# Another order of the work from the last pair's transposes to the first expert slot, and the ranks in two fp32r passes

## The reference, cut to what matters

```
x = x + xattn(layernorm(x), ctx, ctx)        # softmax over 1601 context rows
x = x + attn(layernorm(x))                   # causal, 64 rows of a batch
x = layernorm(x)  -> ffn, added to x:
    top2 of sigmoid(x @ centroids.T + bias) over 8 experts, softmax of the two scores
    shared: 2 experts, gelu(x @ Wfc.T) @ Wproj.T
    routed: 8 experts, the same, weighted by the gates
```

## Time and profile before

| | |
|---|---|
| median of 3 executions | 253.61 us (253.21 to 254.71) |
| the profiled execution | 252.07 us |
| its span, first to last instruction | 250.3 us |
| outside the span | 1.8 us |
| TensorE busy | 242.9 us, 97% |
| VectorE, ScalarE, GpSimd busy | 61%, 55%, 20% |

### The profile page before, as it was taken

One profiled execution on the slowest core, in us unless ns is written; L12 is line 12 of the kernel. 1 busy time (PEld: TensorE's weight loads), 2 busy tenths in 40 slices (PEclk: granted clock), 3 DMA queues, 4 the chain that ended last, 5 costly groups with the idle time before them and its releaser, 6 DMA issues.

```text
span 250.3 us, 5122 instructions
## 1 busy us (share of the span) xinstructions
PE 242.9 (97%) x1908; PEld 209.6 (84%) x1908; DVE 152.4 (61%) x365; ACT 137.2 (55%) x271; POOL 50.6 (20%) x81
## 2 busy tenths in 40 slices
PE   7999999999999999999998999999999999999994
PEld 6857646366467599999998899999999999999994
DVE  1722246545635788788759147666766766667683
ACT  0725206052152688796776166666666666666641
POOL 5100000000100010420686002102122222226700
PEclk9999999999999999999999999999999999999999
DMA  7999999999999999930166358999989999920132
GB/s 249 425 432 402 417 415 427 384 405 429 351 376 385 352 347 429 427 143 0 67 187 261 101 152 283 373 356 369 370 346 358 363 360 364 335 107 21 56 135 84
DMA packets 13870, 74.12 MB, mean 296 GB/s; under 512 B 1524, under 2 KB 8444, under 8 KB 9500
## 3 DMA queue, kind: packets, MB, share of 16 engines
q1 hardware_dynamic: 12700, 70.59, 74.4%
q0 software_dynamic: 1008, 2.76, 2.9%
q10 hardware_dynamic: 144, 0.53, 0.6%
HBM read 67.56 MB, written 6.32 MB: 295 GB/s over the span
## 4 chain that ended last, share of the span: by engine, by line
PE 72%; DMA 15%; POOL 3%; DVE 3%; ACT 3%; issue 2%; SPq 1%; POOLq 0%; DVEq 0%; ACTq 0%
PE psum L512 64%; DMA raw<-experts_dram 9%; PE psum L760 4%; POOL slot_x_dram L479 3%; DMA slot_x_dram<-second,rows_of 3%; DMA squares<-squares_dram 2%; PE psum L601 1%; PE psum L778 1%; DMA xrow<-slot_x_dram 1%; ACT prob L885 1%; PE psum L821 1%; DVE xn L1046 1%; PE psum L552 0%; PE psum L650 0%; PE psum L692 0%
## 5 line engine op out<-in xcount | busy, mean ns | idle before, releaser
L512 PE MATMUL psum<-xrowT,ring 128*128 128x128 f32 x480 | 58.3, 275 | 0.0
L512 PEld LDWEIGHTS psum<-xrowT,ring 128*128 128x128 f32 x480 | 56.2, 192 | 0.0
L1301 DVE TENSOR_TENSOR dlo<-ring,dhi 128x1024 fp32r<-128x1024 f32 x30 | 38.4, 1281 | 3.7 <-ACT dhi L968 3.7
L1320 DVE TENSOR_TENSOR slot_hlo<-slot_h,slot_hhi 128x512 fp32r<-128x512 f32 x30 | 20.8, 692 | 30.0 <-ACT slot_hhi L996 30.0
L994 ACT ACTIVATE slot_h<-psum 128x512 f32<-128x512 f32 x30 | 18.0, 600 | 35.7 <-PE psum L512 35.7
L512 PE MATMUL psum<-dhi,slot_hhi 128*128 128x256 f32 x120 | 36.3, 302 | 0.1
L512 PE MATMUL psum<-dhi,slot_hlo 128*128 128x256 f32 x120 | 33.8, 282 | 0.0
L512 PE MATMUL psum<-dlo,slot_hhi 128*128 128x256 f32 x120 | 33.8, 282 | 0.0
L968 ACT ACTIVATE dhi<-ring 128x1024 fp32r<-128x1024 f32 x30 | 31.1, 1040 | 0.0
L504 POOL DMA_INDIRECT results_dram<-y_rows,result_row x13 | 15.6, 1199 | 71.8 <-DMA results_dram<-y_rows,result_row 55.3
L512 PE MATMUL psum<-xh,parted 128*128 128x256 f32 x128 | 26.8, 286 | 0.1
(11 more groups left out here) (195 smaller groups left out, 408.2 us busy)
## 6 DMA issues: line engine op xcount, KB each, us to landing
ring<-experts_dram SPq DMA_DIRECT2D x15, 2048.0 KB, 8.2
ctx<-ctx_dram SPq DMA_DIRECT2D x4, 3072.0 KB, 24.5
ctxT_start<-ctxT_start_dram SPq DMA_DIRECT2D x4, 2048.0 KB, 19.0
ctxT_rest<-ctxT_rest_dram SPq DMA_DIRECT2D x4, 1154.0 KB, 21.8
raw<-experts_dram SPq DMA_DIRECT2D x2, 2048.0 KB, 16.4
slot_x_dram<-empty_row SPq DMA_DIRECT2D x1, 1935.0 KB, 16.9
xrow<-slot_x_dram SPq DMA_DIRECT2D x15, 129.0 KB, 7.1
squares<-squares_dram SPq DMA_DIRECT2D x1, 1285.0 KB, 14.2
```

What stands on the lines that cost most here:

```text
L512: return pe.matmul(out, lhsT, rhs, start=first, stop=last)
L1301: dve.tensor_tensor(dlo[b % 2][:, steps, :], ring[b][:, steps, C * P:STEP_W], dhi[b % 2][:, steps, :].bitcast(F32), ALU.subtract).then_inc ...
L1320: dve.tensor_tensor(slot_hlo[:, half, :], slot_h[:, half, :], slot_hhi[:, half, :].bitcast(F32), ALU.subtract).then_inc(slot_hlo_ready, 1)
```

## The change

The removed part of the list stands in plan() above and is left out of the diff. The second half of the list, from pair 3's transposes to the first slot, is written in another order. "split" 0 stands ahead of pair 3's transposes, where it stood behind pair 2's projection; the value products W of pair 3 are cut at other places and end later in the list. Units, norms and routing entries change places by a few positions. SyncE's and GpSimd's programs keep their order, apart from three constants on GpSimd. The ranks are computed in two fp32r matmuls, the first over the running sums (with the total as a fifth block of 8 columns), the second over the choices; before, they were three fp32 matmuls.

```
--- before.py
+++ after.py
@@ -79,30 +79,30 @@
                   ("exp", t + 1, 2), ("exp", t + 1, 3), *([] if t else [("x_bias", )]), ("W", t, 3 if t else 4, KT)]
 
     t, c, late = T - 1, T - 2, T - 3
...
+    order += [("split", 0), ("T", t, 0), ("T", t, 1), ("mixT", c), ("probT", late), ("T", t, 2), ("z", late),
+              ("T", t, 3), ("proj", c), ("split", 1), ("W", t, 0, 1), ("norm2", c), ("norm3", late), ("W", t, 1, 4),
+              ("split", 2), ("W", t, 4, 6), ("split", 3), ("W", t, 6, 7), ("split", 4), ("xn2T", c), ("W", t, 7, 9),
+              ("split", 5), ("xn3T", late), ("tq", c), ("W", t, 9, 10), ("xl", late), ("W", t, 10, 11), ("sc", c),
+              ("W", t, 11, KT), ("split", 6), ("v", c), ("hid", 0), ("mixT", t), ("hid", 1), ("split", 7),
+              ("exp2", c), ("feat", 0), ("proj", t), ("hid", 2), ("hid", 3), ("feat", 1), ("feat", 2), ("probT", c),
+              ("norm2", t), ("down", 0), ("z", c), ("feat", 3), ("xn2T", t), ("split", 8), ("split", 9), ("hid", 4),
+              ("tq", t), ("down", 1), ("hid", 5), ("sc", t), ("norm3", c), ("feat", 4), ("down", 2), ("v", t),
+              ("split", 10), ("exp2", t), ("xn3T", c), ("hid", 6), ("probT", t), ("xl", c), ("route", 0), ("z", t),
+              ("route", 1), ("feat", 5), ("hid", 7), ("down", 3), ("norm3", t), ("split", 11), ("feat", 6),
+              ("down", 4), ("xn3T", t), ("xl", t), ("route", 2), ("down", 5), ("route", 3), ("feat", 7), ("hid", 8),
+              ("rz", ), ("down", 6), ("sigmoid", ), ("top2", ), ("indices", ), ("hid", 9), ("feat", 8), ("hot", ),
+              ("choices", ), ("feat", 9), ("down", 7), ("hid", 10), ("hid", 11), ("feat", 10), ("gap", ), ("down", 8),
+              ("hid", 12), ("feat", 11), ("hid", 13), ("rank", ), ("place", ), ("place_experts", ), ("down", 9),
+              ("place_rows", ), ("hid", 14), ("feat", 12), ("hid", 15), ("down", 10), ("down", 11),
+              ("place_tokens", ), ("gates", ), ("feat", 13), ("feat", 14), ("hid", 16), ("down", 12), ("hid", 17),
+              ("down", 13), ("down", 14), ("split", 12), ("feat", 15), ("feat", 16), ("feat", 17), ("hid", 18),
+              ("down", 15), ("hid", 19), ("down", 16), ("down", 17), ("feat", 18), ("split", 13), ("feat", 19),
+              ("split", 14), ("hid", 20), ("down", 18), ("split", 15), ("feat", 20), ("down", 19), ("hid", 21),
+              ("hid", 22), ("feat", 21), ("hid", 23), ("down", 20), ("slot_down", 0), ("hid", 24), ("feat", 22),
+              ("down", 21), ("down", 22), ("feat", 23), ("hid", 25), ("feat", 24), ("hid", 26), ("down", 23),
+              ("hid", 27), ("slot_down", 1), ("feat", 25), ("down", 24), ("down", 25), ("hid", 28), ("feat", 26),
+              ("feat", 27), ("down", 26), ("slot_rows", ), ("feat", 28), ("hid", 29), ("down", 27), ("down", 28),
+              ("tables", ), ("feat", 29), ("down", 29)]
     return order
 
 
@@ -118,7 +118,8 @@
         ident = sb("ident", [P, P])
         mask = sb("mask", [P, P])
         neghalf = sb("neghalf", [P, T])
-        tri = sb("tri", [P, P])
+        tri = sb("tri", [P, P], F32R)
+        ones_r = sb("ones_r", [P, P], F32R)
         ones = sb("ones", [P, P])
         iota8 = sb("iota8", [P, T, ROUTED])
         iota128 = sb("iota128", [P, ROUTED])
@@ -155,9 +156,8 @@
         idxf = sb("idxf", [P, T, TOP])
         hot = sb("hot", [P, TOP, T, ROUTED])
         gat = sb("gat", [P, TOP, T, ROUTED])
-        chosen = sb("chosen", [P, T, ROUTED])
-        before = sb("before", [P, T, ROUTED])
-        total = sb("total", [P, ROUTED])
+        chosen = sb("chosen", [P, T, ROUTED], F32R)
+        before = sb("before", [P, T + 1, ROUTED], F32R)
         rank = sb("rank", [P, T, ROUTED])
         count = sb("count", [P, ROUTED])
         over = sb("over", [P, 3, ROUTED])
@@ -430,8 +430,8 @@
                                     pattern=[[-1, P]], channel_multiplier=1))
             pool.memset(mask[SQ:P, 0:SQ], MASKED).then_inc(consts, 1)
             pool.wait_ge(consts, 4)
-            link(pool.memset(tri[:, :], 1.0))
-            pool.affine_select(out=tri[:, :], in_=tri[:, :], compare_op=ALU.is_ge, fill=0.0, base=-1,
+            pool.tensor_copy(ones_r[:, :], ones[:, :])
+            pool.affine_select(out=tri[:, :], in_=ones[:, :], compare_op=ALU.is_ge, fill=0.0, base=-1,
                                pattern=[[1, P]], channel_multiplier=-1).then_inc(consts, 1)
             link(pool.memset(empty_row[:, :], 0.0))
             pool.iota(empty_row[:, D:D + 1], pattern=[[0, 1]], base=TOP * N, channel_multiplier=1,
@@ -446,7 +446,7 @@
 
             link(pool.iota(xn[:, :, D], pattern=[[P, T]], base=0, channel_multiplier=1,
                            allow_small_or_imprecise_dtypes=True))
-            link(pool.memset(before[:, 0, :], 0.0))
+            link(pool.tensor_copy(before[:, 0, :], empty_row[:, 0:ROUTED]))
             link(pool.memset(ones8[:, :], 1.0))
             pool.iota(iota8[:, :, :], pattern=[[0, T], [1, ROUTED]], base=0, channel_multiplier=0,
                       allow_small_or_imprecise_dtypes=True).then_inc(consts, 1)
@@ -729,11 +729,10 @@
             def ranks():
 
                 pe.wait_ge(chosen_ready, 1)
+                mm(bank(RANK_BANK, 0, (T + 1) * ROUTED), ones_r[:, :], before[:, :, :].rearrange("p t e -> p (t e)"),
+                   True, False)
                 mm(bank(RANK_BANK, 0, T * ROUTED), tri[:, :], chosen[:, :, :].rearrange("p t e -> p (t e)"),
-                   True, False)
-                mm(bank(RANK_BANK, 0, T * ROUTED), ones[:, :], before[:, :, :].rearrange("p t e -> p (t e)"),
-                   False, True)
-                mm(bank(RANK_BANK, T * ROUTED, ROUTED), ones[:, :], total[:, :], True, True).then_inc(rank_ps, 1)
+                   False, True).then_inc(rank_ps, 1)
 
             def hidden(n, tok):
 
@@ -1222,10 +1221,12 @@
             def choices():
 
                 link(dve.tensor_tensor(chosen[:, :, :], hot[:, 0, :, :], hot[:, 1, :, :], ALU.add))
-                for t in range(1, T):
-                    link(dve.tensor_tensor(before[:, t, :], before[:, t - 1, :], chosen[:, t - 1, :], ALU.add))
-                dve.tensor_tensor(total[:, :], before[:, T - 1, :], chosen[:, T - 1, :], ALU.add
-                                  ).then_inc(chosen_ready, 1)
+                for t in range(1, T + 1):
+                    ins = dve.tensor_tensor(before[:, t, :], before[:, t - 1, :].bitcast(F32),
+                                            chosen[:, t - 1, :].bitcast(F32), ALU.add)
+                    if t < T:
+                        link(ins)
+                ins.then_inc(chosen_ready, 1)
 
             def place():
```

More of the change, by code:

```diff
@@ L81, in plan @@
     t, c, late = T - 1, T - 2, T - 3
[L82 to L105, removed]
```

## The result

The changed kernel takes **260.71 us** (median of 6 runs, 260.34 to 262.22). The kernel before took 253.94 (6 runs, 253.21 to 254.71) on the same chip. The ratio is 1.0279, with a 95% interval of 1.0249 to 1.0308: 6.8 us slower in the medians, 7.1 by the ratio. The forecast was 258.5, its range 255.6 to 260.4. So the direction and the main mechanism (the stall) were right, and the total was too small by 2.2 us, just outside the range.

The account below looks back on a forecast made before the run. TensorE, busy 242.9 of 250.3 us, was taken as the bound. To the median of 253.6 us came +4.1 from the order and ranks and +0.8 for the clock, +4.9 in all: 258.5 us, range 255.6 to 260.4.

Parts of the forecast that it names:

- the stall: Pair 3's transpose group 2 on TensorE waits for ScalarE's copy, held behind split 0 until raw[0] lands: +5.1 us.
- the small waits: TensorE's waits at pair 2's xn2T (-0.3), pair 3's xn3T (+0.3) and before the slots (-0.3, -0.3).
- the ranks: Two small fp32r instructions replace six rank instructions on TensorE: -0.4 us (-0.35 to -0.6).
- the clock: TensorE's clock may fall to half in the idle time ahead of group 2: +0.8 us, bounds 0 and 2.0.
- partial: Rival: raw[0] lands 1 to 3 us earlier, TensorE waits 2 to 4, clock holds; 254.7 to 256.6 us; chance 0.07.
- xn3T of pair 3: TensorE waits for pair 3's last norm, with too few units to fill the time: +0.3 us (0 to 0.6).
- xn2T: TensorE's 0.28 us wait ahead of pair 2's xn2T goes, both norms being done by then: -0.3 us.
- Before the slots: Waits at a down unit (0.65) and slot_rows (0.42) shrink: -0.3 (0 to -0.65) and -0.3 (-0.4 to +0.8) us.
- in time: Rival: raw[0] lands by about 77.3, so split 0 hardly delays group 2; -0.5 to -1.5, 252.5 us; chance 0.07.
- The routing chain becomes the bound: Rival: token rows come later, slot_rows waits 1 to 2 us on top; 260.5 to 261.5 us; chance 0.06.
- the ranks do not get cheaper: Rival: small fp32r rank instructions cost as much as the fp32 ones, +0.4 us on any case; no chance given.

Follow-up runs that it names:

- split 0 taken back: Changed kernel with split 0's list entry moved behind pair 2's proj, no longer ahead of pair 3's transposes; 254.67 us, ratio 1.0069.
- raw[0] first: Changed kernel with the load of raw[0] issued ahead of the last ctx block instead of behind it; 254.92 us, ratio 1.0052.
- the filler: Changed kernel with 17 unused fp32 identity matmuls on TensorE ahead of pair 3's transpose group 2; 259.08 us, ratio 1.0233.
- new head: Kernel before with the new order up to the rank, split 0 behind proj, and fp32r ranks; old order behind the rank; 255.04 us, ratio 1.0028.
- ranks alone: Kernel before in its old order, with only the ranks changed to two fp32r matmuls; 253.46 us, ratio 1.0025.
- new tail: Kernel before with the new order only behind the rank, splits 10 and 11 behind gates, and fp32r ranks; 253.17 us, ratio 0.9966.

## Why the forecast was right in kind and too small

The step that failed is the account of the order outside the stall. The forecast put the small waits and the ranks at -0.3 - 0.4 + 0.3 - 0.3 - 0.3 = -1.0 us; the changed kernel with split 0 taken back, which has all of them, is 1.7 us above the kernel before. That is 2.7 us off. The stall was 1.0 smaller than forecast (4.1 timed against 5.1), the clock 0.2 larger in the medians (about 1 against 0.8), and the kernel before took 0.3 us more in its six runs than the 253.6 that I started from: 2.7 - 1.0 + 0.2 + 0.3 = 2.2, the whole miss. In the profiled execution the clock was mis-sized as well, 2.7 us against 0.8.

The second profile of the kernel before is the better yardstick for the sum, as it has the late waits that 12 of the 13 profiles with all scatters have. Start times of TensorE in it and in three others, and the differences that follow:

| | W of pair 3 | to the rank | rank to slot_rows | slot_rows to last matmul | last matmul |
|---|---|---|---|---|---|
| before, second profile | 80.08 | 33.16 | 27.39 | 106.80 | 247.43 |
| after | 86.22 | 35.02 | 26.91 | 107.51 | 255.66 |
| split 0 taken back | 80.17 | 34.62 | 26.79 | 107.49 | 249.07 |
| raw[0] first | 80.98 | 34.33 | 26.84 | 107.50 | 249.65 |

After against before is +8.23 = 6.14 + 1.86 - 0.48 + 0.71. The 0.71 is no loss: one unit of 0.71 us moved behind slot_rows. The two profiled executions lie 8.24 us apart in time (261.08 and 252.84), the medians 6.8.

- **Split 0 ahead of the transposes, forecast +5.1: 4.4 in the trace, 4.1 timed.** Every step of it happened, and the size was 0.7 to 1.0 too large: the landing (81.22 against 81.86), the split, the copy behind it, group 2 behind that. The transfer was 0.9 us shorter than in the earlier trace rows, with a start 0.2 later. That it could not vanish, and that it would not be partial, held in both profiles of the changed kernel.
- **The clock, forecast +0.8 between 0 and 2.0: 2.7 us in the profiled execution** (1.7 in the second one, about 1 in the medians against the filler, 1.7 against the two executions without a fall). Two errors. I took the price of a fall as four microseconds of work; it was 5.4. And I halved it because one case of a fall proves little; the mean clock was 0.978 to 0.993 in all twelve executions of the changed kernel, and not one kept it whole (a late fall, seen in other kernels, may be all of it in some).
- **xn3T of pair 3, forecast +0.3 (0 to 0.6): 0.70 or 0.71**, in all seven profiles with the new head. From W to the rank the new head costs 34.62 - 33.16 = 1.46 us: this wait, 0.30 ahead of xn2T, and some 0.5 in smaller gaps and spacings that I did not foresee.
- **xn2T, forecast -0.3: this step failed too.** The second profile of the kernel before does not have this wait, so there was nothing to win, and without the stall the new head has it: 0.30 us with split 0 taken back, 0.59 with the new head alone.
- **The ranks, forecast -0.4: 0.45 in the trace, nothing to be seen in the time** (ratio 1.0025 alone). The late wait did not take it up in the trace: it was 2.16 us there and 2.19 in the second profile of the kernel before, and from W to the last matmul the ranks alone need 166.86 us against 167.35. That the timed runs don't show these 0.5 us may come from their more frequent falls of the clock; it is not shown.
- **Before the slots, forecast -0.6 in two terms: this step failed.** I read the 0.65 and the 0.42 as waits that a list could move. Both do disappear, and others take their place. Rank to slot_rows falls by 0.48, where one unit less (0.71) and the ranks (0.45) alone make 1.16: the new order loses 0.7 there. In this stretch the late release of TensorE's results during the scatters makes the waits, and I had not seen it because I had one profile of the kernel before, with none of it.

Against the second profile of before, then: 4.3 for the stall (82.41 against 78.09), 2.6 for the clock (1.8 ahead of W, 0.8 in it), 1.1 for the head (what is left of 1.86), -0.45 for the ranks and +0.7 for the tail, 8.25 in all. In the timed medians: stall 4.1, clock about 1, the rest of the order 1.7 (1.3 by the kernel with raw[0] first, its wait of 0.78 for ctx included). The rivals "in time" and "partial" fell with the landing, at 81.2 in the trace. "The routing chain becomes the bound" fell too: slot_rows has no wait in the changed kernel. That the ranks do not get cheaper fell in the trace. Three readings of the forecast were off by themselves: 1 to 2 us on top of 258.5 are 259.5 to 260.5, not the 260.5 to 261.5 of the routing rival; the terms of the rival "in time" reach down to -1.0 and not to -1.5; and feat 7 stands ahead of rz in the old list too.

**Do the two halves add up?** The ratios don't; the traces do, with one profile each:

| | W to the rank | rank to last matmul |
|---|---|---|
| before, second profile | 33.16 | 134.19 |
| ranks alone | 33.18 | 133.68 |
| new head, fp32r ranks | 34.87 | 135.20, of which a fall of the clock some 1.7 |
| new tail, fp32r ranks | 33.20 | 134.25 |
| split 0 taken back | 34.62 | 134.28 |

The new head costs 1.5 to 1.7 us, the new tail 0.6 over the old one with the same ranks, and the ranks give 0.5; together that is the 1.55 us by which the kernel with split 0 taken back is longer. The ratios differ from this by the falls of the clock: on the chip of the two halves 12 of 23 runs of the kernel before had the lower mean clock, 6 of 12 of the new head, none of the new tail; beside the kernel with split 0 taken back it was 4 of 23, and 2 of its own 12. So behind the old head the new tail costs work and saves falls. Behind the stall it does not save them all: three of the six executions with the filler had one, and the profile shows it at 139.2 to 142.6 us.

**What stays open.** One experiment shows that the second half of the scatters costs 2.2 us; that the late semaphore updates are its path is argued, and by what mechanism a scatter would delay them is open, as is why one profile has none of it. Where the 0.5 us of small gaps in the new head and the 0.6 us of the new tail arise was not tested, nor what makes the clock fall in some executions and not in others.

## What to carry to other kernels

An instruction that waits for a transfer costs nothing at the end of an in-order engine's list and the whole remaining flight in front of a copy that another engine needs: before a preparatory step is moved up, compare its data's landing with its new place, not with its old one. If it has to be early, change the order of the transfers as well; here that one swap won back 5.6 us of 7. Take more than one profile of the kernel before when the forecast rests on waits below 1 us.

## What the runs showed of the hardware

- With an idle stretch of 4.1 to 4.4 us on TensorE the clock went to 0.5 in all four profiles that have it unfilled (from 80.9 to 87.8 us in one execution of the changed kernel, from 83.1 to 86.5 in another); with one of 0.8 us it did not. It is not a certainty: two of the six executions of the new order with the old ranks had a mean clock of 1.0. In the profile with seventeen fp32 matmuls on the identity in the hole it stayed at 1.0 there.
- A wait of 1.6 to 2.4 us late in the kernel also goes with a fall in some executions, as over 133.3 to 136.7 us in the profile of the new head alone, at a wait of 2.40 that ended at 133.58. The two profiles of the old order with a wait of 2.16 and of 2.19 have none. The runs of the kernel before form two groups, near 253.3 us at a mean clock of 0.997 or more, and near 254.6 at 0.991 to 0.993 (252.45 and 254.15 on the first of three chips). Several short waits in its place (0.16 to 0.50 us, the new tail alone) left all 12 executions at 0.998 or more.
- While the indirect scatters run, semaphore updates of TensorE arrive up to 3.85 us after the matmuls' modelled ends in the second profile of the kernel before, three of them within 0.15 us; in the first one none is later than 0.02. With four scatters of eight the longest idle stretch of ScalarE there was 0.92 us against 4.80 and 1.11, and the kernel gained 2.2 us.
- Two fp32r matmuls of 40 and 32 columns take 0.14 us from the first's start to the next unit; their two starts are 0.03 apart.
